# Causal masks of an attention stage: from TensorE products to VectorE additions in PSUM, with half of one evacuation given to ScalarE

## The reference

```python
x = x + 0.5 * ffn(layernorm(x))        # 32 routed experts, 16 anchors, one shared expert
x = x + attn(layernorm(x))             # 16 heads of 64, causal, its own residual
x = x + 0.5 * ffn(layernorm(x))

# inside attn, per sequence:
scores = q @ k.T / sqrt(64)            # 512 x 512 for each of 16 heads
scores = scores + where(causal, 0, -inf)
out    = x + softmax(scores) @ v @ Wo
```

## Time and profile before

| | us |
|---|---|
| median of 3 runs (1437.65 to 1438.94) | 1437.99 |
| the profiled execution, its own time | 1439.19 |
| its span | 1437.2 |

### The profile page before, as it was taken

How to read it: one execution, slowest core, us unless ns; L and a number is a source line. 1 busy time by engine, 2 the same in 40 slices (tenths; PEclk the granted TensorE clock), 3 DMA queues, 4 the chain that set the end, 5 groups by cost and what they waited for, 6 DMA issues and landing times.

```text
span 1437.2 us, 27512 instructions
## 1 busy us (share of the span) xinstructions
PE 1409.8 (98%) x9680; PEld 966.2 (67%) x9680; DVE 1112.1 (77%) x2521; ACT 803.0 (56%) x1909; POOL 288.7 (20%) x586
## 2 busy tenths in 40 slices
PE   5999999999999999999999999999999999999998
PEld 4666666666656667676767676776566666666665
DVE  8888888887777777777777778778777777787775
ACT  4344344433357878787878877877644333323322
POOL 1000000000034444444444444444400000000000
PEclk9999999999999999999999999999999999999999
DMA  6443333333310000000000000000043434343332
GB/s 233 160 131 107 117 98 119 106 114 109 109 41 2 2 2 2 2 2 2 2 2 2 2 2 3 1 2 2 2 133 107 121 106 128 104 126 110 121 113 88
DMA packets 59025, 98.07 MB, mean 68 GB/s; under 512 B 6160, under 2 KB 15504, under 8 KB 58896
## 3 DMA queue, kind: packets, MB, share of 16 engines
q1 hardware_dynamic: 58896, 96.38, 21.7%
HBM read 92.68 MB, written 3.67 MB: 67 GB/s over the span
## 4 chain that ended last, share of the span: by engine, by line
PE 91%; DVE 5%; ACT 1%; issue 1%; POOL 0%; DMA 0%; SPq 0%; POOLq 0%; DVEq 0%; ACTq 0%
PE banks L424 19%; PE banks L199 15%; PE banks L201 14%; PE banks L200 14%; PE banks L562 10%; PE banks L527 9%; PE banks L548 6%; PE banks L383 2%; PE banks L537 2%; PE banks L395 1%; DVE nmax L1311 1%; DVE stage L1326 1%; DVE work L1188 1%; ACT work L867 1%; POOL work L1472 0%
## 5 line engine op out<-in xcount | busy, mean ns | idle before, releaser
L777 ACT ACTIVATE work<-banks 128x512 f32<-128x512 f32 x320 | 191.1, 598 | 445.3 <-PE banks L201 433.7
L424 PE MATMUL banks<-work,wd 128*128 128x512 f32 x672 | 342.6, 593 | 0.4 <-DVE work L1188 0.2
L1197 DVE TENSOR_TENSOR work<-banks,work 128x512 f32<-128x512 f32 x320 | 220.8, 690 | 150.9 <-ACT work L777 146.4
L867 ACT ACTIVATE work<-banks,nmax 128x512 f32<-128x512 f32 (+3 forms) x512 | 264.4, 527 | 40.9 <-DVE nmax L1311 36.0
L1472 POOL TENSOR_SCALAR work<-work,rrec 128x512 f32<-128x512 f32 (+3 forms) x512 | 263.3, 543 | 0.0
L199 PE MATMUL banks<-xT_hi,wg_hi 128*128 128x512 f32 x336 | 248.2, 739 | 0.7 <-DVE wu_lo L1179 0.7
L1188 DVE TENSOR_TENSOR work<-work 128x512 f32<-128x512 f32 x320 | 226.6, 708 | 5.4 <-DMA work<-cw_rows 1.3
L1311 DVE TENSOR_REDUCE nmax<-banks 128x2 f32<-128x1024 f32 (+3 forms) x256 | 195.3, 805 | 3.2 <-PE banks L537 3.2
L1326 DVE COPY stage<-banks 128x1024 f32<-128x1024 f32 (+1 forms) x128 | 121.8, 952 | 40.1 <-PE banks L548 39.8
L424 PEld LDWEIGHTS banks<-work,wd 128*128 128x128 f32 x672 | 126.1, 189 | 34.7 <-DVE work L1188 3.1
L201 PE MATMUL banks<-xT_hi,wg_lo 128*128 128x512 f32 x336 | 133.4, 397 | 0.0
(11 more groups left out here) (140 smaller groups left out, 2188.1 us busy)
## 6 DMA issues: line engine op xcount, KB each, us to landing
work<-cw_rows SPq DMA_DIRECT2D x320, 256.0 KB, 3.1
x<-in_x SPq DMA_DIRECT2D x8, 256.0 KB, 6.5
out_rows<-x SPq DMA_DIRECT2D x8, 256.0 KB, 2.2
cw_rows<-cwT SPq DMA_DIRECT2D x16, 96.0 KB, 1.9
stage<-in_w_gate SPq DMA_DIRECT2D x3, 448.0 KB, 4.7
wd<-in_w_down SPq DMA_DIRECT2D x3, 448.0 KB, 7.8
stage<-in_w_up SPq DMA_DIRECT2D x2, 448.0 KB, 6.4
stage<-in_wq SPq DMA_DIRECT2D x1, 512.0 KB, 4.2
```

The source lines that it names most:

```text
L424: pe.matmul(psY, wd[:, j * P:(j + 1) * P], z[part_slot(j)], start=j == 0, stop=j == HT - 1, skip_group_check=True).then_inc(s["down_ps"], 1)
L777: nc.scalar.activation(silu[j % 2], psG[j % 3], ACT.Silu).then_inc(s["silu_done"], 1)
L867: m = nc.scalar.activation(prob[:, p % 2, i, o:o + w], ps[:, i, so:so + w], ACT.Exp, bias=nmax[:, p % 2, i, qb:qb + 1], accum_out=rsum[:, ...
L1197: tt(gated[j % 3], psU[j % 3], silu[j % 2], ALU.mult).then_inc(s["gated_done"], 1)
```

## The change

- `scores` on TensorE loses the mask products. The wait that stood between the two halves of the mask products (`transposes_ready`) now stands ahead of the third of the score products of the last block of a unit.
- A new VectorE function `mask_scores` adds the mask in place in PSUM, on 2 x 128 columns for u=0 and u=1 and on 2 x 256 for u=2. It signals `masked`; `row_max` waits for that.
- In the VectorE slot each maximum is preceded by its `mask_scores`, and the maximum of u=1 moves behind `k_lo`.
- Group 0 of the transposed probabilities is copied half by VectorE and half by ScalarE; ScalarE does its half between exp u=1 and exp u=2. The counts of `pT_act` follow (three for each pair, not two), and TensorE waits for that copy ahead of the transposes of group 1.
- The mask is one float32 tile of 128 x 128, loaded by a DMA that is issued after the second `load_down`; `half`, its load and its cast go.

```diff
@@ sync @@
-            sp.dma_start(half_f32, small_in[:, SMALL:]).then_inc(s["half_loaded"], 16)
             load_group(sp, 1)
             load_down(sp, 0)
             load_down(sp, 1)
+            sp.dma_start(mask[:, :], small_in[:, SMALL:]).then_inc(s["mask_loaded"], 16)
@@ tensor, scores @@
                 for qb, o, w in blocks:
+                    final = qb in (3, 2, 0)
                     for k, (a, c) in enumerate(((0, 0), (0, 1), (1, 0))):
+                        if k == 2 and final and transposes_ready is not None:
+                            transposes_ready()
                         for i in (0, 1):
                             r = slice(i * DK, (i + 1) * DK)
-                            pe.matmul(ps[:, i, o:o + w], qk[0][a][r, p % 2, qb * P:(qb + 1) * P],
-                                      qk[1][c][r, p % 2, 0:w], start=qb != 0 and k == 0, stop=False,
-                                      skip_group_check=True)
-
-                o, w = ((3 * P, P), (2 * P, P), (P, 2 * P))[u]
-                for k in (0, 1):
-                    if k == 1 and transposes_ready is not None:
-                        transposes_ready()
-                    for i in (0, 1):
-                        r = slice(i * DK, (i + 1) * DK)
-                        m = pe.matmul(ps[:, i, o:o + w], half[r, k * P:(k + 1) * P],
-                                      half[r, 2 * (k + 1) * P:2 * (k + 1) * P + w], start=False,
-                                      stop=k == 1, skip_group_check=True)
+                            m = pe.matmul(ps[:, i, o:o + w], qk[0][a][r, p % 2, qb * P:(qb + 1) * P],
+                                          qk[1][c][r, p % 2, 0:w], start=qb != 0 and k == 0,
+                                          stop=final and k == 2, skip_group_check=True)
                 m.then_inc(s["s_ps"], 1)
@@ tensor, attn_slot @@
                 def second_ready():
                     if not (first and p == 0):
                         pe.wait_ge(s["norm_done"], 8 * n)
                         pe.wait_ge(s["pT_dve"], 2 * n - 1)
+                        pe.wait_ge(s["pT_act"], 3 * n - 2)
@@ scalar @@
-                dst, src = transposed(p, g, slice(2 - g, 2))
+                dst, src = transposed(p, g, slice(1 if g < 2 else 0, 2))
                 nc.scalar.activation(dst, src, ACT.Copy).then_inc(s["pT_act"], 1)
@@ scalar, attn_slot @@
                     exp(*ahead(b, p, 1), 1, False)
+                pT_copy(b, p, 0, first and p < 2)
+                if have_s:
                     exp(*ahead(b, p, 1), 2, False)
@@ vector, first chunk @@
-                        dve.wait_ge(s["half_loaded"], 16)
-                        nc.vector.tensor_copy(half[:, :], half_f32).then_inc(s["half_ready"], 1)
-                        dve.wait_ge(s["half_ready"], 1)
@@ vector @@
+            def mask_scores(b, p, u):
+                n = pair(b, p)
+                dve.wait_ge(s["s_ps"], 3 * n + u + 1)
+                if n == 0 and u == 0:
+                    dve.wait_ge(s["mask_loaded"], 16)
+                o, w = ((3 * P, P), (2 * P, P), (P, 2 * P))[u]
+                ps = score_banks(p, u)[:, :, o:o + w].rearrange("p i (b c) -> p i b c", c=P)
+                tt(ps, ps, mask[:, :].unsqueeze(1).unsqueeze(1).broadcast_to([P, 2, w // P, P]), ALU.add) \
+                    .then_inc(s["masked"], 1)
             def row_max(b, p, u):
                 n = pair(b, p)
-                dve.wait_ge(s["s_ps"], 3 * n + u + 1)
+                dve.wait_ge(s["masked"], 3 * n + u + 1)
@@ vector, pT_copy @@
-                nc.vector.tensor_copy(*transposed(p, g, slice(0, 2 - g))).then_inc(s["pT_dve"], 1)
+                nc.vector.tensor_copy(*transposed(p, g, slice(0, 1))).then_inc(s["pT_dve"], 1)
@@ vector, attn_slot @@
                 if have_s:
                     row_rec(b, p)
                 if have_s:
+                    mask_scores(*ahead(b, p, 1), 0)
                     row_max(*ahead(b, p, 1), 0)
-                    row_max(*ahead(b, p, 1), 1)
+                    mask_scores(*ahead(b, p, 1), 1)
                 ...
                 if have_q:
                     part_lo(*ahead(b, p, 2), 1, False)
+                if have_s:
+                    row_max(*ahead(b, p, 1), 1)
                 if have_q:
                     part_lo(*ahead(b, p, 2), 0, False)
                 if have_s:
+                    mask_scores(*ahead(b, p, 1), 2)
                     row_max(*ahead(b, p, 1), 2)
```

More of the change, by code:

```diff
@@ L62, in constants @@
     mask = np.where(np.arange(P)[None, :] > np.arange(P)[:, None], NEG, 0.0)
-    halves = [np.tile(m[i * DK:(i + 1) * DK], (2, 1)) for m in (ident, mask) for i in (0, 1)]
-    halves = halves[0:2] + [halves[2], halves[2], halves[3], halves[3]]
     iota = np.broadcast_to(np.arange(E, dtype=np.float32)[None, :], (P, E))
     tie = np.broadcast_to((np.arange(G)[None, :] < np.arange(G)[:, None]), (P, TB, G, G))
-    small = np.concatenate([ident, iota, tie.reshape(P, -1), *halves], 1)
+    small = np.concatenate([ident, iota, tie.reshape(P, -1), mask], 1)
     return small.astype(np.float32)
@@ L94, in build @@
         tie = small[:, P + E:].rearrange("p (t a b) -> p t a b", t=TB, a=G)
-        half = sb("half", [P, 6 * P], BF16)
+        mask = sb("mask", [P, P])
         gate_w = sb("gate_w", [P, E])
@@ L113, in build @@
         spread = work[:, 10 * CH:].rearrange("p (k c) -> p k c", k=NSPREAD)
-        half_f32 = work[:, 5 * CH:5 * CH + 6 * P]
         prob = work[:, 0:4 * PW].rearrange("p (r i c) -> p r i c", r=2, i=2)
@@ L170, in build @@
         psT, psA, psO = pairs[2], bank[6], bank[7]
-        names = """small_loaded gate_loaded half_loaded half_ready attn_w_loaded
+        names = """small_loaded gate_loaded mask_loaded attn_w_loaded
             stat_dve stat_act stat_rows stat_bn rsqrt
@@ L179, in build @@
             a_xn a_xT_ps a_xT_hi a_xT_lo a_xres
-            q_ps k_ps v_ps q_hi q_lo k_hi k_lo v_sb s_ps max_done exp_done rec_done norm_done
+            q_ps k_ps v_ps q_hi q_lo k_hi k_lo v_sb s_ps masked max_done exp_done rec_done norm_done
             pT_ps pT_act pT_dve ctx_ps ctx_hi ctx_lo out_ps outT_sb outT_ps out_added stored""".split()
@@ L555, in attend @@
                 pe.wait_ge(s["pT_dve"], 2 * n + 2)
-                pe.wait_ge(s["pT_act"], 2 * n + 2)
+                pe.wait_ge(s["pT_act"], 3 * n + 3)
                 pe.wait_ge(s["v_sb"], b * HP + (TB if p < TB else HP))
@@ L600, in third_ready @@
                         pe.wait_ge(s["pT_dve"], 2 * n)
-                        pe.wait_ge(s["pT_act"], 2 * n - 1)
+                        pe.wait_ge(s["pT_act"], 3 * n - 1)
                 def first_ready():
@@ L606, in first_ready @@
                     else:
-                        pe.wait_ge(s["pT_act"], 2 * n)
+                        pe.wait_ge(s["pT_act"], 3 * n)
                     if have_q:
@@ L715, in attention @@
                 pe.wait_ge(s["pT_dve"], 2 * NC * HP - 1)
+                pe.wait_ge(s["pT_act"], 3 * NC * HP - 2)
                 probT(NC - 1, HP - 1, 1)
@@ L720, in attention @@
                 pe.wait_ge(s["pT_dve"], 2 * NC * HP)
-                pe.wait_ge(s["pT_act"], 2 * NC * HP - 1)
+                pe.wait_ge(s["pT_act"], 3 * NC * HP - 1)
                 probT(NC - 1, HP - 1, 2)
@@ L1402, in attention @@
             def attention():
+                mask_scores(0, 0, 0)
                 row_max(0, 0, 0)
+                mask_scores(0, 0, 1)
                 row_max(0, 0, 1)
@@ L1407, in attention @@
                 part_lo(0, 1, 0, True)
+                mask_scores(0, 0, 2)
                 row_max(0, 0, 2)
```

## The result

The changed kernel takes 1499.57 us (median of 6 runs, 1498.8 to 1501.87), the kernel before 1437.82 beside it: a ratio of 1.0428 with a 95% interval of 1.0416 to 1.044. The forecast was 1497 us. The profiled span is 1498.1 us, 60.9 more than before.

What follows compares the result with a forecast made beforehand. A VectorE-ScalarE wait loop replaces TensorE's list as bound: 8.43 + 0.46 + 0.87 + 0.73 = 10.49 us a slot, 0.93 over the average; 58.6 us over 63 distances, +59 with the edges, median 1497 us, range 1474 to 1522.

Steps and rivals of the forecast that it cites:

- a loop of waits through VectorE and ScalarE: Attention slot: from maximum u=2 round to itself, 8.43 us before the change and 10.49 after, replacing TensorE's list as bound.
- The additions: VectorE's mask additions in PSUM: 0.42 us each for u=0 and u=1, 0.69 for u=2.
- The wait on the addition: VectorE: an addition its maximum waits for costs full duration plus 0.04 us, 0.46 for u=0 and 0.73 for u=2.
- The maximum of u=1: VectorE: moved between `k_lo` and `q_lo`, it stands on the loop and costs 0.87 us a slot.
- sign of 85 to 88% busy: Sign of being right: TensorE 85 to 88% busy in attention, waiting for exps, `k_lo`, `q_lo` or copies.
- the faster rival: Attention: TensorE stays the bound and gives back 0.50 us a slot, -31 us, time 1406; chance 0.04.
- The split copy: Group 0's copy: VectorE's part falls from 1.21 to 0.69 us, off the loop; ScalarE's 0.49 hidden with 0.65 to spare.
- The edges: Outside the slots: +0.8 us ahead of the first reciprocal, -0.5 from the first chunk's lost cast and load.
- The average: Attention: a slot costs 0.93 us more than the average of 9.56; 63 distances make 58.6 us.
- dearer additions: VectorE's additions at their upper bounds: 0.52 us a slot more, 33 us, time 1530; half of that, 1513; chance 0.10.
- a free wait: VectorE: a maximum's wait on its addition costs nothing, 0.24 us a slot, 15 us less, time 1482; chance 0.13.
- a lower clock: TensorE's granted clock falls in attention, priced at 0.4 us a slot, 25 us, time 1522; chance 0.10.

Runs made afterwards that it cites:

- e2: Changed kernel with the reciprocal moved between the addition for u=0 and its maximum; 1493.4 us, against 1499.6 for the changed kernel.
- e1: Changed kernel with the maximum of u=1 back in its old place ahead of `k_lo`; 1473.9 us, against 1499.6 for the changed kernel.
- e4: Changed kernel with TensorE adding its mask products as well, so the mask is added twice; 1499.1 us, against 1499.6 for the changed kernel.
- e7: Kernel before with no causal mask on the diagonal blocks, on TensorE or VectorE; 1426.3 us, against 1437.8 for the kernel before.
- e3: Changed kernel with group 0 copied by VectorE alone again, additions kept; 1521.6 us, against 1499.6 for the changed kernel.
- e10: Kernel before with only the mask of u=2 on VectorE, group 0 copied by VectorE alone; 1464.6 us, against 1437.8 for the kernel before.
- e11: Kernel before with only the mask of u=2 on VectorE and group 0 copied half by VectorE, half by ScalarE; 1440.9 us, against 1437.8 before.
- e8: Kernel before with only the mask of u=1 moved to VectorE, between the maxima of u=0 and u=1; 1433.7 us, against 1437.8 before.
- e9: Kernel before with only the mask of u=0 moved to VectorE; 1456.3 us, against 1437.8 for the kernel before.

## Why the prediction was right, step by step

The mechanism and the size were right: a loop of waits through VectorE and ScalarE, 10.49 us by the sum and 10.48 in the trace, takes the place of TensorE's list. That the two numbers agree to 0.01, and the forecast with the measured time to 3 us, is in part luck, as the points below show.

- *The additions*: 0.42 and 0.69 us forecast; measured 0.415 and 0.690. `k_lo` and `ctx_lo`, which write 512 elements to SBUF, take 0.692 and 0.690:

```profile
L1304 DVE TENSOR_TENSOR banks<-banks,mask 128x256 f32<-128x256 f32 x92 | 38.2, 415 | 0.0
...
L1304 DVE TENSOR_TENSOR banks<-banks,mask 128x512 f32<-128x512 f32 x45 | 31.1, 690 | 0.0
```

- *The wait on the addition*: 0.46 and 0.73 forecast from start to start; 0.44 and 0.73 measured (712.24 to 712.68, 717.98 to 718.71), and e2 shows that the wait itself costs. The Trainium skill (VectorE: DVE Perf Modes, "The DRAIN you can't avoid") says that a semaphore after each operation costs nothing extra; here, where the next operation waits for it, filling the wait brought 0.105 us a slot.
- *Two small misses that cancel*: the maximum of u=0 reads 1.23 us, not the 1.17 of the earlier trace rows, where it follows its addition, so its exp comes after 1.26 and not 1.21. From exp u=2 to `ctx_hi` it is 1.59 (709.29 to 710.88) and not 1.64. In the kernel before `ctx_hi` started 0.04 us after the end of the product with the values (700.41 + 2.38 = 702.79, and 702.83), so the 1.64 seems to hold a short wait for TensorE.
- *The maximum of u=1*: 0.87 forecast, 716.52 to 717.38 measured. e1 shows that its place decides over nearly 26 us.
- *TensorE's slack*: e4 shows that its lost 0.50 us count nothing in the changed kernel. The prediction's sign of 85 to 88% busy was missed: it is 91%, and the busy time for each slot did not fall, as said above. And "that is all that TensorE can give back", 1406 us as the faster rival's time, was too good: e7 gives 1426. The step that failed is the list of loops. I followed one and took 8.43 us for the shortest possible slot behind TensorE; a second one, over `q_lo` and the product with the values, was at 9.27, and the first with `q_hi` in it at 8.85. The forecast stood because the second loop stayed below the first in the changed kernel too, which the prediction did not look at: `ctx_lo` could have started 0.61 us after the copy at 710.70 and started at 711.52, so what comes over that copy, the second loop included, had only 0.21 us to spare: about 10.27 us.
- *The split copy*: "not on the loop, and the 0.52 us gained are worth nothing there" is true only of what is left after it. e3 shows that without the split the change would have cost 22 us more, and e10 against e11 shows nearly the same in another kernel, 24 us. The prediction compared the copy with exp u=2 and `ctx_hi` and stopped at the copy's end; it had to go on over the transposes that wait for it. The 1.2 us to spare that it gave the copies left these transposes out. ScalarE's half is hidden as forecast: it still waits 0.54 us for the maximum of u=2.
- *The edges*: up to the first reciprocal the forecast was +0.8 - 0.5 = +0.3 us, and +0.8 was measured. The first FFN gains 0.3 us and not 0.5 (its last layer norm starts at 407.15, before at 407.45), and from there to the first reciprocal it is 1.1 us more and not 0.8. The 1.2 us less behind the last reciprocal were not foreseen. They offset a part of the 2.7 and 0.5 us that the slots and the start took beyond the forecast, and the median lies 0.35 us under the profiled time and not 1.2.
- *The average*: a slot grew by 0.97 and not 0.93. The rest is the work done once a chunk (10.53 on average, 10.48 for a plain slot), for which the prediction allowed 0.05 and added nothing.
- *The upper bounds of the additions*: half as long again would be 0.63 and 1.03, not the 0.68 and 0.95 given; nothing measured came near either.
- *The rivals*: dearer additions and a free wait are ruled out by the rows, a lower clock by the granted 1.00 with TensorE busy 436.64 of 480 us. What the Trainium skill (TensorE: Matmul & The Clock Gate, "HAM oscillation — how this bites in real kernels") says of repeated idle gaps does not show at the gaps of about 0.5 us in this kernel; longer ones, no run tried.

## What to carry to other kernels

Where several engines hand work round in a fixed order, the free share of an engine says little: add up each closed way through the waits, from one instruction to the same one a slot later, and compare it with the fullest engine. Follow every branch until it comes back, also through the full engine itself, and don't take a busy share near 100% as a sign that the engine never waits (e7). Work moved off a full engine paid here only in a place where the receiver waits for something anyway (e8); an addition of the same size two places earlier in the same list cost 1.3% (e9).

## What the runs showed of the hardware

VectorE adds in place in PSUM in 415 ns for 256 elements of each partition and 690 for 512; the latter is what the two-operand operations that write to SBUF take (692 and 690). An operation that waits for the one ahead of it on VectorE starts 0.03 to 0.04 us after its end (712.68, 718.71), one that doesn't about 0.08 before it (717.98); filling that place with an independent operation of 0.19 us won 0.105 us a slot (e2).
